# Adding expert outputs to token rows in DRAM inside the expert loop, tile by tile

## The reference, cut to what matters

```
shared = silu(xf @ sg) * (xf @ su) @ sd                 # every row
top_idx, gates = the 4 best of 32 experts per row, softmax of their scores
pos = place of the row in its expert's list; keep = pos < 320
buf[e, pos] = xf[row]                                   # 320 rows an expert, the rest zero
h = silu(buf @ wg) * (buf @ wu);  out_e = h @ wd        # per expert
routed[row] += out_e[e, pos] * gate * keep              # 4 contributions a row
out = x + shared + routed
```

## Time and profile before

| | |
|---|---|
| median of 3 runs | 1864.75 us (1864.67 to 1867.48) |
| the profiled execution's own time | 1868.67 us |
| its span, first to last instruction | 1867.0 us |
| mean granted clock | 0.931 |
| busy in the span: PE, DVE, ACT, POOL | 1544.0, 1014.4, 798.5, 887.1 us |
| last output tile out of PSUM (end of L1382) | 1769.7 us |

### The profile page before, as it was taken

One profiled execution on the slowest core, in us unless ns is written; L12 is line 12 of the kernel. 1 busy time (PEld: TensorE's weight loads), 2 busy tenths in 40 slices (PEclk: granted clock), 3 DMA queues, 4 the chain that ended last, 5 costly groups with the idle time before them and its releaser, 6 DMA issues.

```text
span 1867.0 us, 25548 instructions
## 1 busy us (share of the span) xinstructions
PE 1544.0 (83%) x7946; PEld 1085.8 (58%) x7946; DVE 1014.4 (54%) x1423; ACT 798.5 (43%) x1543; POOL 887.1 (48%) x775
## 2 busy tenths in 40 slices
PE   2799999999999999999999996441999999999800
PEld 2455555655555555455555554331789999999800
DVE  5456556556555565655655555710366666666533
ACT  2345344444444544445444444200256666666500
POOL 4356657666665675766666572175000101101175
PEclk8899999999999999999999997575999999999955
DMA  9000000000000000000000001022055555555237
GB/s 305 13 16 18 1 21 13 0 21 12 7 14 12 12 8 12 12 8 12 12 10 11 12 1 68 1 102 78 8 185 188 173 164 184 172 169 184 69 104 121
DMA packets 82412, 118.25 MB, mean 63 GB/s; under 512 B 7940, under 2 KB 56775, under 8 KB 82375
## 3 DMA queue, kind: packets, MB, share of 16 engines
q1 hardware_dynamic: 72647, 90.52, 15.6%
q0 software_dynamic: 9728, 27.28, 5.3%
HBM read 77.29 MB, written 31.46 MB: 58 GB/s over the span
## 4 chain that ended last, share of the span: by engine, by line
PE 60%; issue 13%; POOL 12%; DVE 7%; ACT 4%; another core or an unknown queue 1%; DMA 1%; POOLq 0%; DVEq 0%; ACTq 0%; SPq 0%
PE ps_o L720 9%; PE ps_t L634 9%; PE ps_m L634 7%; POOL arena L548 7%; PE ps_st L634 7%; PE ps_m L685 6%; PE ps_st L705 4%; PE ps_o L816 4%; PE ps_m L816 4%; PE ps_t L740 3%; PE ps_st L709 3%; POOL arena L598 3%; ACT arena L1301 2%; POOL arena L553 2%; PE ps_t L834 2%
## 5 line engine op out<-in xcount | busy, mean ns | idle before, releaser
L548 POOL TENSOR_TENSOR arena<-arena 128x512 f32<-128x512 f32 (+1 forms) x512 | 655.9, 1282 | 395.8 <-ACT arena L1301 368.3
L1301 ACT ACTIVATE arena<-ps_st 128x512 f32<-128x512 f32 (+1 forms) x576 | 326.0, 595 | 453.4 <-PE ps_st L709 442.0
L1002 DVE TENSOR_REDUCE arena_r<-ps_m 128x1 fp32r<-128x1101 f32 x256 | 332.1, 1297 | 306.1 <-PE ps_m L685 305.8
L705 PE MATMUL ps_st<-arena_r 128*128 128x512 f32 (+1 forms) x576 | 263.0, 457 | 23.1 <-ACT arena L1301 23.0
L720 PE MATMUL ps_o<-arena 128*64 128x512 f32 (+1 forms) x1152 | 268.4, 601 | 0.0
L582 POOL DMA_DIRECT2D y_slots<-arena x32 | 23.2, 726 | 437.1 <-ACT arena L1382 343.8
L709 PE MATMUL ps_st<-arena_r 68*128 68x512 f32 (+2 forms) x576 | 228.8, 397 | 0.9 <-DVE arena_r L1009 0.9
L634 PE MATMUL ps_m<-arena_r 128*128 128x320 f32 (+1 forms) x864 | 162.9, 324 | 68.9 <-issue 44.5
L685 PE MATMUL ps_m<-arena_r 128*128 128x512 f32 (+1 forms) x768 | 193.2, 360 | 5.4 <-DVE arena_r L1002 5.4
L685 PEld LDWEIGHTS ps_m<-arena_r 128*128 128x128 f32 x768 | 137.6, 191 | 91.0 <-issue 44.6
L634 PEld LDWEIGHTS ps_m<-arena_r 128*128 128x128 f32 x864 | 137.2, 191 | 75.9 <-issue 50.8
(11 more groups left out here) (144 smaller groups left out, 1899.8 us busy)
## 6 DMA issues: line engine op xcount, KB each, us to landing
arena<-in_L_ffn_wg_dram SPq DMA_DIRECT2D x32, 512.0 KB, 3.6
arena<-in_L_ffn_wu_dram SPq DMA_DIRECT2D x32, 512.0 KB, 4.7
arena<-in_L_ffn_wd_dram SPq DMA_DIRECT2D x32, 512.0 KB, 6.4
x_slots<-zeros SPq DMA_DIRECT2D x1, 10240.0 KB
arena_r<-arena_r SPq DMA_DIRECT2D x32, 275.2 KB, 3.6
arena<-x_slots SPq DMA_DIRECT2D x32, 256.0 KB, 2.7
y_slots<-arena POOLq DMA_DIRECT2D x32, 256.0 KB, 5.5
x_sb<-in_x_dram SPq DMA_DIRECT2D x2, 1024.0 KB, 7.3
```

Of the source, the lines that this page charges most:

```text
L548: pool.tensor_tensor(acc, probsT[0:rows, h, 0, :] if kt == 1 else acc, probsT[0:rows, h, kt, :], ALU.add).then_inc(added, 1)
L705: pe.matmul(ps_st[0:rows, n % 2, :], k1[b][h][:, r], q1[h][:, c:c + 512], start=True, stop=False)
L1002: dve.tensor_reduce(neg[h][:, c:c + 1], scores_m[:, 0:KEYS], AX.X, ALU.max, negate=True)\
L1301: act.activation(probsT[0:rows, h, kt, :], ps_st[0:rows, n % 2, :], ACT.Exp)\
```

## The change

Instead of storing expert outputs to `y_slots` and gathering them at the end, a DRAM tensor `acc` holds the token rows. SP fills it with `x_sb` chunk by chunk as the shared feed-forward ends. POOL adds each output tile to it by an indirect DMA with an add, as soon as ACT has copied that tile out of PSUM. For this each row in `x_slots` is 272 floats wide, not 256: it carries its token number (`TOK`), its 4 gates and its 4 expert numbers. After its hidden activations DVE reads these fields for the 320 rows of the expert (`slot_gates`) and makes the destination numbers `ids` and the gate of each row, by which ACT scales the output tile. Spare slots point at rows behind the tokens; they are filled at the start out of `fill` (64 partitions). At the end SP copies `acc` to the output, DRAM to DRAM. The core of the diff:

```
-    yslots = nc.dram_tensor("y_slots", [SLOTS + 1, D], ...)
+    acc = nc.dram_tensor("acc_rows", [NTOK + CAP, D], ...)       # x_slots rows: D + 16 wide
 SP, start:
-            sp.dma_start(xslots[0:SLOTS, :]..., zeros[:, :] ...).then_inc(init_out, 16)
+            for j in range(FJ):                                  # 5 times
+                sp.dma_start(acc[NTOK + j * FP:NTOK + (j + 1) * FP, :], fill[:, j, 0:D])
+                sp.dma_start(spare[j], fill[:, j, :].unsqueeze(1).broadcast_to([FP, E, RW]))
 SP, before the loop:
+            for c in range(NCHUNK):
+                for i in (2, 3):
+                    job_done(sp, J_SHARED + i, c * 2)
+                sp.dma_start(acc[c * 512:(c + 1) * 512, :]..., x_sb[:, c * 4:c * 4 + 4, :])
 SP, feed:
                 sp.wait_ge(job_ready[1], (J_EXPERT // 2 - 2 + 1) + e)
+                sp.wait_ge(ids_done, e * 2 + 2)
                 sp.dma_start(xg[par] ...)                        # rows, then the weights
 SP, end:
+            sp.wait_ge(add_out, 16 * CTL * E)
             for b in range(B):
-                sp.wait_ge(summed, (b + 1) * QT_N)
-                sp.dma_start(out[b]..., x_sb[...])
+                sp.dma_start(out[b], acc[b * S:(b + 1) * S, :])
 POOL:
+            pool.wait_ge(init_out, 32 * FJ)                      # ahead of the attention's sums
+            def add(par, turn):
+                e = turn * 2 + par
+                for c, (_, rows) in enumerate(CAP_TILES):
+                    pool.wait_ge(ysb_ready, e * CTL + c + 1 + 2)
+                    pool.indirect_dma_start(out=acc[:, :], in_=y_sb[par][0:rows, c, :],
+                        compute_op=ALU.add, out_offset=... ids[0:rows, par, c:c + 1] ...)
+                pool.wait_ge(add_out, (e + 1) * 16 * CTL)
+                pool.sem_inc(ysb_free, 1)
-            (store, and the 64 gathers of L598)
 DVE:
+            dve.sem_inc(ids_done, 4)                             # once, at the start
+            def slot_gates(par, turn):
+                e = turn * 2 + par
+                dve.wait_ge(rows_in[par], turn * 32 + 32)
+                dve.wait_ge(ysb_free, e + 1)
+                dve.tensor_copy(ids[:, par, 0:CTL], xg[par][:, :, TOK]).then_inc(ids_done, 1)
+                dve.scalar_tensor_tensor(picks, xg[par][:, :, IDS:IDS + TOPK], iota_e[:, bass.ds(e, 1)],
+                                         xg[par][:, :, GATES:GATES + TOPK], is_equal, mult)
+                dve.wait_ge(picked_up, e + 1)
+                dve.tensor_reduce(slot_gate[:, par, :], picks, AX.X, ALU.add).then_inc(ids_done, 1)
 DVE, expert: after hidden(...), before rows_lo(...):
+                slot_gates(par, turn)
 DVE, router: three small writes of TOK, IDS, GATES; the two that made yslot are gone
-            (the 64 multiply-adds of L1219)
 ACT, y_out:
-                    act.activation(y_sb[...], ey_bank[...], ACT.Copy)
+                    act.activation(y_sb[...], ey_bank[...], ACT.Copy, scale=slot_gate[0:rows, par, c:c + 1])
+                act.wait_ge(ids_done, (turn * 2 + par) * 2 + 6)  # once, before the first tile
```

More of the change, by code:

```diff
@@ L328, in xattn_moe @@
         rows_in = [sem(f"rows_in{i}") for i in range(2)]
-        ystore_out = sem("ystore_out")
-        yg_in = [sem(f"yg_in{i}") for i in range(YRING)]
+        acc_in, add_out = sem("acc_in"), sem("add_out")
+        ids_done, picked_up = sem("ids_done"), sem("picked_up")
         copies_in = [sem(f"copies_in{i}") for i in range(B)]
@@ L496, in _ @@
             seq = Chain(pool, pool_seq)
-            seq.done(pool.memset(zeros[:, :], 0.0))
+            seq.done(pool.memset(fill[:, :, :], 0.0))
             seq.done(pool.memset(ident[:, :], 0.0))
@@ L575, in _ @@
                         out_offset=bass.IndirectOffsetOnAxis(ap=slot[:, t, k:k + 1].bitcast(U32), axis=0),
[L576 to L578 removed]
+                        in_=h_row[:, t, :], in_offset=None).then_inc(xslots_out, 16)
+            pool.wait_ge(acc_in, 16 * NCHUNK)
+            def add(par, turn):
                 e = turn * 2 + par
[L580 to L587, removed]
+                for c, (_, rows) in enumerate(CAP_TILES):
+                    pool.wait_ge(ysb_ready, e * CTL + c + 1 + 2)
+                    pool.sem_inc(pool_step, 1)
+                    pool.indirect_dma_start(
+                        out=acc[:, :], in_=y_sb[par][0:rows, c, :], in_offset=None, compute_op=ALU.add,
+                        out_offset=bass.IndirectOffsetOnAxis(ap=ids[0:rows, par, c:c + 1].bitcast(U32), axis=0))\
+                        .then_inc(add_out, 16)
+                pool.wait_ge(add_out, (e + 1) * 16 * CTL)
                 pool.sem_inc(ysb_free, 1)
             with pool.Fori(0, E // 2) as i:
[L591 to L601, removed]
+                add(0, i)
+                add(1, i)
         @block.tensor
@@ L1143, in _ @@
             seq.done(dve.tensor_scalar(keep[:, :, :], posk[:, :, :], float(CAP), None, ALU.is_lt))
+            seq.done(dve.tensor_copy(h_row[:, :, IDS:IDS + TOPK], topf[:, :, :]))
+            seq.done(dve.tensor_scalar(h_row[:, :, TOK], dropslot[:, :, 0], -float(SLOTS), 1.0 / TOPK, ALU.add, ALU.mult))
+            seq.wait()
             seq.done(dve.tensor_scalar(topf[:, :, :], topf[:, :, :], float(CAP), None, ALU.mult))
@@ L1154, in _ @@
             seq.wait()
-            dve.sem_inc(slots_ready, 1)
-            seq.done(dve.tensor_tensor(posk[:, :, :], posk[:, :, :], dropslot[:, :, :], ALU.add))
-            seq.wait()
-            seq.done(dve.tensor_scalar(yslot[:, :, :], posk[:, :, :], float(SLOTS), None, ALU.min))
+            seq.done(dve.tensor_copy(h_row[:, :, GATES:GATES + TOPK], gate[:, :, :]))
             seq.wait()
@@ L1214, in _ @@
             expert(1, E // 2 - 1, False)
-            for t in range(NT):
-                dve.wait_ge(yg_in[t % YRING], 16 * TOPK * (t // YRING + 1))
-                for k in range(TOPK):
-                    seq.done(dve.scalar_tensor_tensor(x_sb[:, t, :], yg[:, t % YRING, k, :], gate[:, t, k:k + 1],
-                                                      x_sb[:, t, :], ALU.mult, ALU.add))
-                    seq.wait()
-                dve.sem_inc(summed, 1)
         @block.scalar
@@ L1381, in y_out @@
                     act.wait_ge(ey_ready, turn * (2 * CTL) + par * CTL + c + 1)
-                    act.activation(y_sb[par][0:rows, c, :], ey_bank[(par * CTL + c) % 2][0:rows, 0:D], ACT.Copy)\
+                    act.activation(y_sb[par][0:rows, c, :], ey_bank[(par * CTL + c) % 2][0:rows, 0:D], ACT.Copy,
+                                   scale=slot_gate[0:rows, par, c:c + 1])\
                        .then_inc(ysb_ready, 1)
```

50 lines of the change are left out of this document (32 added, 18 removed).

## The result

| | median | runs | ratio to before, 95% |
|---|---|---|---|
| kernel before | 1866.12 us | 4 (1864.67 to 1868.23) | |
| changed kernel | 1912.87 us | 4 (1912.6 to 1921.37) | 1.0261 (1.023 to 1.0291), slower |

The change costs 46.8 us, where +27 was forecast (1892 us, range 1845 to 1955). The profiled execution of the changed kernel took 1921.37 us, with a span of 1919.5 us; the other three had spans of 1910.7 to 1911.1 us. Its ledger is therefore some 8 us dearer than the median.

A forecast was written before the change was run, and what follows sets the result against it. The prediction took PE to bound the expert loop. Its terms, +1 + 0.5 + 2.3 + 103 - 80 = +27 us on the median 1864.75, gave 1892 us, range 1845 to 1955.

The forecast's parts named there:

- up to the experts' first group: Before the expert loop: +1 us for the fill, +0.5 for DVE writes, +2.3 for the copy of chunk 3.
- 30 rounds: Expert loop, experts 2 to 31: each round 16.25 us instead of 12.83, +103 us in all, bounds +47 and +182.
- tail: After the last output tile: stores, gathers and gated additions go, 97.3 us become 16.7; -80 us used.
- The mechanism: SP's queue: waiting for slot_gates delays rows and weights, so ACT waits; the lateness repeats each expert, 12.83 to 16.25 us.
- G: Expert loop: the end of slot_gates, put 0.6 us behind DVE's last low part; weights were needed 5.2 us later.
- The landing: Expert loop: weights land 8.45 us after slot_gates, bounds 7.5 and 10, which is 3.3 us late.
- Landing to slot_gates: Expert loop: from weights landed through ACT, DVE and PE to the end of slot_gates, 7.05 us before any clock loss.
- The pause and the clock: Before PE's group 3: a 2.7 us pause each expert lets the clock fall, adding 0.75 us a round (0 to 1.7).
- the ring: Expert loop: transfers land, hidden activations finish, slot_gates, next transfers; 15.5 us a round, 16.25 with the clock.
- Weights soon enough: Rival, expert loop: adds take nothing from the weights and the clock holds; round 14.4 us, time 1836 us, chance 0.13.
- The wait hidden entirely: Rival, expert loop: weights arrive within 5.2 us of slot_gates; round stays 12.83 us, time 1789 us, chance 0.03.
- The additions hold the DMA engines: Rival, expert loop: adds delay the weights to 10 us after slot_gates; round 18.9 us, time 1971 us, chance 0.12.

The follow-up runs named there:

- e5: The changed kernel once more, unedited, on another chip than its first profile: 1917.85 us, 1.0279 of the kernel before.
- e1: The kernel before with only a wait in SP's feed for the hidden activations of expert e - 2, ahead of rows and weights: 1947.87 us, ratio 1.0421.
- e2: The changed kernel with the weights issued ahead of the wait for slot_gates and the rows behind it: 1799.06 us, ratio 0.9616.
- e9: The changed kernel with the indirect additions left out, so the output lacks the experts' shares: 1891.3 us, ratio 1.0136.
- e3: The changed kernel with plain indirect writes in place of the indirect additions: 1923.68 us, ratio 1.0293.
- e11: The changed kernel with the wait still ahead of the weights, but the weights issued before the two row transfers: 1853.13 us, ratio 0.9928.
- e7: The changed kernel with the expert rows filled from 128 partitions, not 64: 1913.05 us, ratio 1.0255.
- e6: The changed kernel with 16 idle matmuls of 320 columns ahead of PE's group 3 of each expert: 1906.03 us, ratio 1.021.
- e10: The changed kernel without the indirect additions and with 16 idle matmuls of 320 columns ahead of group 3: 1874.41 us, ratio 1.0038.

## Why the prediction was right, and where its sizes were off

Three terms of the sum, against both profiles of the changed kernel:

| | predicted | first profile | e5 |
|---|---|---|---|
| up to the experts' first group | +3.8 | 1366.26 - 1357.78 = +8.5 | 1361.53 - 1357.78 = +3.8 |
| 30 rounds | +103 (3.42 each) | (1904.63 - 1366.26) - (1769.73 - 1357.78) = +126.4 (4.2 each) | (1893.54 - 1361.53) - 411.95 = +120.1 (4.0 each) |
| tail | -80 | 14.9 - 97.3 = -82.4 | 14.3 - 97.3 = -83.0 |
| sum | +27 | +52.5 | +40.8 |

The sums are the differences of the spans to 1867.0; by the medians the change costs 46.8. The term that was mis-sized is the 30 rounds, by 23 us in the first profile and 17 in e5.

**The mechanism was right.** The wait for `slot_gates` holds the weights in SP's queue, the weights hold quarter 0, and the round repeats it. The chain shows each link, e1 shows the wait making most of the loss alone, e2 shows the loss gone with the order alone. One reading was off and enters no term: the weights go out 10.5 us later than before (G at 1574.54 plus 1.45, against 1565.44), not 8 to 9.

**The landing.** `slot_gates` to wg issue was put at 1.45 us and is 1.51. From there to quarter 0 the prediction had 8.45 + 0.1 - 1.45 = 7.1; it is 7.6. This term was mis-sized by 0.5 us, or 15 us in all. e9 shows that the additions are this half microsecond: without them it is 7.16. The price I had taken from a plain store beside gathers held for the wait alone, not for indirect writes issued beside the weights. The additions make single rounds late by 2 us and leave others as they are. e3 shows that plain indirect writes do the same.

**Landing to slot_gates.** Predicted 6.95 and 0.75 for the clock. It is 6.85 to 6.90 with the clock held, and 0.8 more in e5 (7.67), 1.1 in the first profile (7.99). Over all rounds the two profiles differ by 0.26 us a round, 7.8 us of the 11.7 between their spans (1919.5 and 1907.8); most of the rest lies ahead of the loop. With these values a round is 1.51 + 7.6 + 7.7 = 16.8, against 16.25.

**The pause and the clock.** At the start the clock was at 1.00 in a pause of just under 3 us; in the loop it was at 0.50 behind one of 2.53 us. So that row was no bound for the loop, and taking a value well above 0 in spite of it was right. Nor does the length of the one pause decide: group 3 ran at 1.00 behind 2.58 us of idle PE in e11, and at 0.50 behind 2.27 us in the changed kernel (first and second row). What else decides was not followed.
```profile
1739.30 1.15 PE L643 MATMUL ps_m<-arena_r 128*128 128x320 f32 x6 [2.58 <-DVE arena L1182]
```
```profile
1729.45 1.97 PE L643 MATMUL ps_m<-arena_r 128*128 128x320 f32 x6 [2.27 <-DVE arena L1182]
```

**The start.** +1 was taken for the fill, with bounds 0 and +8, and its rate was the lower one (202 GB/s). The product behind the key copies was 4.1 us late (73.25, and 73.15 in e5), and e7 gives 4.15 back. I should have given more weight to the one row that had 64 partitions in it, which by itself asked for 8: half of that came. Behind the shared feed-forward it took 7.6 us to the first group, not 5.0: +2.6, where 2.3 was worked out for the copy of chunk 3. That e5's sum for the start is the +3.8 of the forecast is luck all the same. From the first scatter to the end of the shared feed-forward the kernel before needed 140.9 us (1211.86 to 1352.77), the changed kernel 139.0 (1219.65 to 1358.62) and 137.5 in e5 (1216.32 to 1353.86); nothing in the prediction makes this stretch shorter, and no run shows what does. Over the nine profiles of kernels with this start the first group begins 2.5 to 10.8 us later than before.

**The rest.** `slot_gates` takes 0.5 us (0.6). SP issues the two output copies at 1910.12, where the last addition was forecast to have landed 6.3 us behind the last tile (1911.0), and a copy takes 7.1 us from issue to landing, where 1.3 and 8 were put for both. POOL's additions come every 1.86 us, not 1.25, and this costs nothing, as e3 shows. ACT's scale was put at nothing; under the ring it is hidden, but in e2, where PE bounds again, it is 0.08 us an expert, some 2.5 us in all.

**The rivals.** Weights soon enough: its landing of G + 7.5 was not seen even without additions (e9: 1.51 + 7.16 - 0.1 = 8.6). The wait hidden entirely: e2 is what it would have looked like, at 1799, 10 us over the 1789 worked out for it, with the late start. The additions hold the DMA engines: they do make the weights later, but by 0.5 us where this rival had 1.55 over the forecast; of 30 rounds of the first profile two were longer than its 18.9 us. Open are what makes single landings late by 2 us (indirect writes, adding or plain, are needed for it, but which of them meets which weight packets was not followed), the late shift in e6, and the shorter stretch behind the scatter.

## What to carry to other kernels

A wait that is put into an in-order issue queue delays all that stands behind it: write down what is queued behind, when each of those is needed, and whether its lateness feeds back into the wait. If it does, the loop's period is the length of that ring, and each microsecond in it counts once an iteration, plus what a falling clock adds; what does not need the wait is issued ahead of it, here for 6.5% of the kernel.

## What the runs showed of the hardware that was not expected

- An indirect addition to DRAM occupies POOL for 1.55 us and comes every 1.86 us, a plain indirect write of the same rows 0.98 and 1.28. In the time of this kernel they are the same.
- Three indirect writes, 320 rows together, beside plain loads of 1.57 MB made the time from the loads' issue to their first use vary from 6.9 to 9.9 us; without them it was 6.8 to 7.7 in e9 and 6.8 to 8.1 in e10.
- While the fill ran at 202 GB/s, single issues of it on SP took up to 9.04 us; at 353 GB/s they took up to 5.47. An issue row of SP is then no sign of SP's own work, and all behind it in the queue is late.
- The copy from DRAM to DRAM was faster than any transfer of the kernel before: 721 and 328 GB/s in two windows of 1 us are the 1.05 MB of the first copy, moved in under 2 us, where the best window of 1 us in the kernel before has 418 GB/s (1544 to 1545). The prediction had put 8 us of data for the two; both are over by 1916, 5.9 us behind the first issue, and data move in only four of the windows of 1 us until then.
